# Dequantisation of three weight matrices ordered by matrix, on one core of a Trainium2

## What is computed

```python
BLOCKSIZE = 64
...
def nf4_quant_dequant(w):
    shape = w.shape
    flat = w.reshape(-1, BLOCKSIZE)
    absmax = jnp.max(jnp.abs(flat), axis=1, keepdims=True)
    normalized = flat / jnp.where(absmax == 0, 1.0, absmax)
    bounds = (NF4_CODE[:-1] + NF4_CODE[1:]) * 0.5
    idx = jnp.searchsorted(bounds, normalized)
    return (NF4_CODE[idx] * absmax).reshape(shape)
dq1 = nf4_quant_dequant(w1)
dq2 = nf4_quant_dequant(w2)
dq3 = nf4_quant_dequant(w3)
gate = jnp.einsum('bsd,hd->bsh', x, dq1)
up = jnp.einsum('bsd,hd->bsh', x, dq2)
h = jax.nn.silu(gate) * up
return jnp.einsum('bsh,dh->bsd', h, dq3)
```

## Time and profile before

| | |
|---|---|
| median of 3 runs (lowest to highest) | 1632.03 us (1629.77 to 1635.35) |
| the profiled execution: its own time | 1631.09 us |
| its span from first to last instruction | 1629.4 us |
| PE busy | 1390.0 us, 85% of the span |
| DVE busy | 1010.8 us, 62% |
| ACT, POOL busy | 461.3 us, 294.3 us |
| mean granted TensorE clock | 0.925 |

### The profile page before, as it was taken

The page is one execution under the profiler, slowest core; times in us unless marked ns, Lnnn a source line. Parts: engine busy times, 40 slices in busy tenths (PEclk is TensorE's granted clock), DMA queues, the critical chain, the costliest instruction groups (busy, mean ns, idle before and its releaser), DMA issues.

```text
span 1629.4 us, 18357 instructions
## 1 busy us (share of the span) xinstructions
PE 1390.0 (85%) x6285; PEld 1070.1 (66%) x6285; DVE 1010.8 (62%) x2281; ACT 461.3 (28%) x993; POOL 294.3 (18%) x170
## 2 busy tenths in 40 slices
PE   5559999999899988989967678589997777888998
PEld 5437776777677766867745467457886454677886
DVE  3657777767877765654596665854457399744141
ACT  3224334332333432313332103223212232321010
POOL 3101111111111111211112002115422311022110
PEclk9879999999999999999976789779998899899999
DMA  5521223313222321132101102100111100011001
GB/s 178 181 73 53 77 62 99 80 53 91 74 55 72 94 78 53 53 87 78 44 26 59 54 21 80 49 18 26 52 52 53 39 0 1 1 39 65 23 19 52
DMA packets 99405, 96.37 MB, mean 59 GB/s; under 512 B 13138, under 2 KB 72418, under 8 KB 99314
## 3 DMA queue, kind: packets, MB, share of 16 engines
q1 hardware_dynamic: 98802, 94.35, 19.8%
q0 software_dynamic: 512, 0.85, 0.2%
HBM read 84.34 MB, written 10.82 MB: 58 GB/s over the span
## 4 chain that ended last, share of the span: by engine, by line
PE 65%; DVE 23%; issue 5%; ACT 3%; DMA 2%; SPq 1%; POOL 1%; DVEq 0%; ACTq 0%; POOLq 0%
PE bank L1666 49%; PE bank L2033 6%; PE bank L1758 4%; DVE nf_y L1611 3%; DVE st L1174 2%; PE bank L1691 2%; DVE xn L1192 1%; PE bank L1748 1%; DVE mx L1528 1%; DMA nf_a<-in_L_w 1%; DVE xT L1151 1%; PE bank L1996 1%; DVE rt L1161 1%; SPq L771 1%; POOL slots L817 1%
## 5 line engine op out<-in xcount | busy, mean ns | idle before, releaser
L1666 PE MATMUL bank<-xT,slots 128*128 128x512 f32 (+1 forms) x1920 | 468.8, 402 | 12.3 <-DVE xT L1151 8.9
L1666 PEld LDWEIGHTS bank<-xT,slots 128*128 128x128 f32 (+1 forms) x1920 | 355.5, 186 | 111.6 <-issue 9.3
L817 POOL TENSOR_TENSOR slots<-staging,slots 128x1024 fp32r<-128x1024 f32 (+4 forms) x97 | 228.3, 2357 | 1063.9 <-ACT slots L910 1063.9
L1611 DVE TENSOR_SCALAR nf_y<-nf_w 128x512 fp32r<-128x512 f32 (+2 forms) x495 | 250.0, 532 | 38.4 <-PE bank L2033 37.2
L1666 PE MATMUL bank<-slots,h 128*128 128x512 f32 (+1 forms) x728 | 179.3, 406 | 15.9 <-DVE h L1284 9.7
L2033 PE MATMUL bank<-nf_y,nf_d 128*128 128x512 f32 (+2 forms) x495 | 165.3, 418 | 13.4 <-DVE nf_y L1611 11.3
L1666 PEld LDWEIGHTS bank<-slots,h 128*128 128x128 f32 (+1 forms) x728 | 141.1, 194 | 51.9 <-DVE h L1284 10.5
L910 ACT ACTIVATE slots<-staging 128x1024 fp32r<-128x1024 f32 (+4 forms) x97 | 98.2, 1018 | 188.6 <-PE bank L1666 175.6
L944 ACT ACTIVATE e<-bank,mx 128x320 f32<-128x320 f32 x128 | 66.4, 523 | 231.5 <-DVE mx L1229 217.9
L2033 PEld LDWEIGHTS bank<-nf_y,nf_d 128*128 128x128 f32 (+1 forms) x495 | 93.6, 194 | 50.4 <-issue 18.0
L1758 PE MATMUL bank<-eT,v 128*96 128x256 f32 (+1 forms) x384 | 108.6, 404 | 0.3
(11 more groups left out here) (246 smaller groups left out, 1716.1 us busy)
## 6 DMA issues: line engine op xcount, KB each, us to landing
staging<-in_L_wqkT SPq DMA_DIRECT2D x16, 480.0 KB, 3.9
nf_out<-nf_w SPq DMA_DIRECT2D x30, 256.0 KB, 2.1
staging<-nf_out SPq DMA_DIRECT2D x30, 256.0 KB, 2.9
staging<-in_L_woT SPq DMA_DIRECT2D x16, 384.0 KB, 3.7
staging<-in_L_w SPq DMA_DIRECT2D x12, 512.0 KB, 3.7
nf_a<-nf_max SPq DMA_DIRECT2D x40, 128.0 KB, 3.5
nf_r<-nf_rcp SPq DMA_DIRECT2D x40, 128.0 KB, 3.3
nf_w<-in_L_w SPq DMA_DIRECT2D x15, 256.0 KB, 4.2
```

The source lines that it names most:

```text
L817: g.tensor_tensor(lo, split_source(i), hi.bitcast(FP32), ALU.subtract).then_inc(*sig.mark("weight_low", i))
L1611: v.tensor_scalar(nf_y[0:rows, i % STAIR_RING, 0:size], w_, bound, first, compare, ALU.mult)\
L1666: ins = mm(dst, l_, r_, start=i == 0, stop=i == len(passes) - 1)
```

## The change

Only the 11 maxima of matrix 0 come first, then `nf_turn` 0 and item 0. The items run matrix by matrix (item n is matrix n // 11, block n % 11). From item 4 on, after its parts 4, 9 and 14, one entry of a second list is put in: the 11 maxima and the turn of matrix 1, then those of matrix 2. Their rows go through `xn[:, 0:3]` with waits three blocks back, their tables lie in `xn[:, 3]`. One copy per matrix is dropped (L1587), and the table is cleared per matrix. SP waits for the stored maxima of an item's own matrix. `stats` (1, 0) waits for the last tables to be stored.

```diff
--- before.py
+++ after.py
@@ -92,6 +92,7 @@
 STAIRS = staircase()
 NPART = len(STAIRS)
 STAIR_RING, STAIR_LAG = 6, 4
+REST_FROM = 4
 NF_BANK = 7
 
 
@@ -379,7 +380,7 @@
         nf_a = sb("nf_a", [P, 2, D], FP32, nfs)
         nf_r = sb("nf_r", [P, D], FP32, nfs)
         l = ExitStack()
-        nf_m = sb("nf_m", [P, 3, 88], FP32, l)
+        nf_m = sb("nf_m", [P, 2, 88], FP32, l)
         nf_t = sb("nf_t", [P, 2, P], FP32, l)
         l.close()
         nf_y = sb("nf_y", [P, STAIR_RING, D], F32R, nfs)
@@ -517,7 +518,7 @@
         def ffn_up(name, gate, up, lo, hi):
             for f in range(lo, hi):
                 w = fwidth(f)
-                chunk((name, f), P, (2, KT, w), [((0,), gate(f)), ((1,), up(f))], after=after_nf(name, 3 * f + 1))
+                chunk((name, f), P, (2, KT, w), [((0,), gate(f)), ((1,), up(f))], after=after_nf(name, FT + f))
 
         def ffn_down(name, down, lo, hi):
             for f in range(lo, hi, 2):
@@ -525,10 +526,10 @@
                 w = fwidth(f + n - 1)
                 if w == P or n == 1:
                     chunk((name, f), w, (n, D), [((i,), down(f + i, w)) for i in range(n)],
-                          after=after_nf(name, 3 * (f + n - 1) + 2))
+                          after=after_nf(name, 2 * FT + f + n - 1))
                 else:
-                    chunk((name, f), P, (1, D), [((0,), down(f, P))], after=after_nf(name, 3 * f + 2))
-                    chunk((name, f + 1), w, (1, D), [((0,), down(f + 1, w))], after=after_nf(name, 3 * f + 5))
+                    chunk((name, f), P, (1, D), [((0,), down(f, P))], after=after_nf(name, 2 * FT + f))
+                    chunk((name, f + 1), w, (1, D), [((0,), down(f + 1, w))], after=after_nf(name, 2 * FT + f + 1))
 
         def after_nf(name, item):
             return ("nf4_stored", item) if name in ("up3", "down3") else None
@@ -579,11 +580,13 @@
         base = schedule(only)
         if only is None or only == 7:
             jobs = []
-            for m in range(3):
+            jobs += [("nf_max", 0, f) for f in range(FT)] + [("nf_turn", 0)]
+            rest = []
+            for m in range(1, 3):
                 for f in range(FT):
-                    jobs += [("nf_max", m, f)] + [("nf_turn", m - 1)] * (m > 0 and f == 4)
-            jobs.append(("nf_turn", 2))
-            items = [(3 * f + m, m, f) for f in range(FT) for m in range(3)]
+                    rest.append(("nf_max", m, f))
+                rest.append(("nf_turn", m))
+            items = [(m * FT + f, m, f) for m in range(3) for f in range(FT)]
             jobs.append(("nf_load", *items[0]))
             sums = []
             for n, m, f in items:
@@ -600,8 +603,12 @@
                         jobs.append(("nf_store", *items[n - 1]))
                     if j == NPART // 2 + 1 and n + 1 < len(items):
                         jobs.append(("nf_load", *items[n + 1]))
+                    if n >= REST_FROM and j % 5 == 4 and rest:
+                        jobs.append(rest.pop(0))
             jobs += sums + [("nf_end", *items[-1]), ("nf_store", *items[-1])]
             base = with_background(base, "v0", BACKGROUND_END, jobs)
+            assert base.index(("turn", 0, 1)) < base.index(("nf_max", 1, 0))
+            assert base.index(("nf_turn", 2)) < base.index(("stats", 1, 0))
         steps = []
         if known:
             last = known.last_step
@@ -680,7 +687,21 @@
 
         def rows_buffer(i):
 
-            return (nf_w, nf_a)[i // 2 % 2][:, i % 2]
+
+
+            return (nf_w, nf_a)[i // 2 % 2][:, i % 2] if i < FT else xn[:, (i - FT) % 3]
+
+        def rows_loaded(i):
+
+            return f"nf4_rows{i % 4 if i < FT else 4 + (i - FT) % 3}"
+
+        def maxima(m):
+
+            return nf_m if m == 0 else xn[:, 3, 0:176].rearrange("p (a n) -> p a n", a=2)
+
+        def turned(m):
+
+            return nf_t if m == 0 else xn[:, 3, 176:432].rearrange("p (a n) -> p a n", a=2)
 
         def stair(n, j):
 
@@ -719,15 +740,17 @@
                 w = fwidth(f) if m < 2 else P
                 n = D if m < 2 or f < 10 else 6 * BLOCK
                 i = m * FT + f
-                if i >= 4:
-                    sp.wait_ge(*sig.when("nf4_max", divmod(i - 4, FT)))
+                if FT <= i < FT + 3:
+                    sp.wait_ge(*sig.when("turn_product", (0, 1, KT - 1)))
+                elif i >= 4:
+                    sp.wait_ge(*sig.when("nf4_max", divmod(i - (4 if i < FT else 3), FT)))
                 src = nf_src[m][f * P:f * P + w] if m < 2 else a["L3_w3"][:, f * D:f * D + n]
-                sp.dma_start(rows_buffer(i)[0:w, 0:n], src).then_inc(*sig.mark(f"nf4_rows{i % 4}", (m, f), 16))
+                sp.dma_start(rows_buffer(i)[0:w, 0:n], src).then_inc(*sig.mark(rows_loaded(i), (m, f), 16))
 
             def nf_turned(m):
                 for i, dst in enumerate((nf_max[m], nf_rcp[m])):
                     sp.wait_ge(*sig.when("nf4_turned", (m, i)))
-                    sp.dma_start(dst, nf_t[0:88, i]).then_inc(*sig.mark(f"nf4_maxima_stored{i}", m, 16))
+                    sp.dma_start(dst, turned(m)[0:88, i]).then_inc(*sig.mark(f"nf4_maxima_stored{i}", m, 16))
 
             def broadcast_rows(dst_tile, src, m, f):
 
@@ -755,10 +778,10 @@
             def nf_load(n, m, f):
                 w = fwidth(f)
                 rows, size = (P, KT * w) if m < 2 else (w, D)
-                if n == 0:
+                if f == 0:
                     for i in range(2):
-                        sp.wait_ge(*sig.when(f"nf4_maxima_stored{i}", 2))
-                else:
+                        sp.wait_ge(*sig.when(f"nf4_maxima_stored{i}", m))
+                if n:
                     sp.wait_ge(*sig.when("nf4_scaled", n - 1))
                 if n >= 2:
                     sp.wait_ge(*sig.when(f"nf4_stored{n % 2}", n - 2))
@@ -1117,11 +1140,11 @@
             def nf_turn(m):
                 for i in range(2):
                     act.wait_ge(*sig.when("nf4_turn_product", m))
-                    if m:
+                    if m > 1:
                         act.wait_ge(*sig.when(f"nf4_maxima_stored{i}", m - 1))
                     elif i == 0:
                         act.wait_ge(*sig.when("nf4_max", (0, 0)))
-                    sc.activation(nf_t[0:88, i], psum(("nf_turn", m))[0:88, i * P:(i + 1) * P], ACT.Copy)\
+                    sc.activation(turned(m)[0:88, i], psum(("nf_turn", m))[0:88, i * P:(i + 1) * P], ACT.Copy)\
                         .then_inc(*sig.mark("nf4_turned", (m, i)))
 
             handlers = {"split": split, "turn": turn, "v0": v0_, "k0": k0_, "kc0": kc0_, "q0": q0_, "scores0": scores0,
@@ -1188,6 +1211,9 @@
                 if layer or hf:
                     prev = (layer, 0, KT - 1) if hf else (layer - 1, 1, KT - 1)
                     dve.wait_ge(*sig.when("turn_product", prev))
+                if (layer, hf) == (1, 0):
+                    for i in range(2):
+                        dve.wait_ge(*sig.when(f"nf4_maxima_stored{i}", 2))
                 for t in ts:
                     v.tensor_scalar(xn[:, t % TPH], x[:, t], mv[:, t, 0:1], rs[:, t:t + 1], ALU.subtract, ALU.mult)\
                         .then_inc(*sig.mark("normalised", (layer, t)))
@@ -1574,19 +1600,17 @@
                 w = fwidth(f) if m < 2 else P
                 n = D if m < 2 or f < 10 else 6 * BLOCK
                 i = m * FT + f
-                dve.wait_ge(*sig.when(f"nf4_rows{i % 4}", (m, f)))
-                if (m, f) == (0, 0):
-                    link(v.memset(nf_m[:], 0.0))
-                v.tensor_reduce(nf_m[0:w, 0, f * 8:f * 8 + n // BLOCK], rows_buffer(i)[0:w, 0:n].rearrange("p (b k) -> p b k", k=BLOCK),
+                dve.wait_ge(*sig.when(rows_loaded(i), (m, f)))
+                if f == 0:
+                    if m > 1:
+                        dve.wait_ge(*sig.when("nf4_turn_product", m - 1))
+                    link(v.memset(maxima(m)[:, 0], 0.0))
+                v.tensor_reduce(maxima(m)[0:w, 0, f * 8:f * 8 + n // BLOCK], rows_buffer(i)[0:w, 0:n].rearrange("p (b k) -> p b k", k=BLOCK),
                                 AX.X, ALU.max, apply_absolute_value=True).then_inc(*sig.mark("nf4_max", (m, f)))
                 if f == FT - 1:
                     dve.wait_ge(*sig.when("nf4_max", (m, f)))
-                    c = 88 if m < 2 else 86
-                    if m:
-                        dve.wait_ge(*sig.when("nf4_turn_product", m - 1))
-                    link(v.tensor_copy(nf_m[:, 1, 0:88], nf_m[:, 0, 0:88]))
-                    link(v.tensor_scalar(nf_m[:, 2, 0:88], nf_m[:, 1, 0:88], TINY, None, ALU.max))
-                    v.reciprocal(nf_m[:, 2, 0:88], nf_m[:, 2, 0:88]).then_inc(*sig.mark("nf4_rcp", m))
+                    link(v.tensor_scalar(maxima(m)[:, 1], maxima(m)[:, 0], TINY, None, ALU.max))
+                    v.reciprocal(maxima(m)[:, 1], maxima(m)[:, 1]).then_inc(*sig.mark("nf4_rcp", m))
 
             def nf_stairs():
 
@@ -2019,7 +2043,7 @@
```

(2 more changed lines are left out.)

## The result

The changed kernel takes 1649.19 us (median of 4 runs, 1646.25 to 1650.66); the kernel before took 1630.9 beside it. The ratio is 1.0107, with a 95% interval of 1.0083 to 1.0132: slower by 17 to 18 us; the profiled spans differ by 17.0, 1629.4 to 1646.4.

What follows compares the result with a forecast made beforehand. PE bounds the attention stage; from 40 to 120 us it idles 34.5 us, waiting for DVE. The terms, -14.5 + 8 - 1 + 14 = 6.5, taken as 6, give 1637.1 us profiled, 1638.0 median; range 1622 to 1650.

Steps and rivals of the forecast that it cites:

- the forecast case: Whole kernel: the predicted outcome, slower at 1638.0 us; case 1634 to 1645 with chance 0.43, own range 1632 to 1645.
- term 2: Units 12 to 36: DVE waits for late row loads, mostly borne; 8 us more, bounds 0 to 25.
- Term 1: The start, before unit 12: early idle time of PE, then fewer waits and sums done ahead; 14.5 us less, bounds 8 to 20.
- the faster case: Rival: start gives 19 as PE keeps its clock, term 2 is 2, Term 3 is 10; -7, 1625 us, chance 0.23.
- The wait behind `stats` (0, 1): At the start: PE's idle time of 8.6 us there falls to 3 to 4, since PE has other work.
- The eight waits behind `nf_store`: Items 4 to 11, maximum after part 4: its load follows the store; DVE idles 2 to 4 us each, 16 to 25 in sum.
- An item's two other row loads go out early and are hidden.: Units 12 to 36: row loads other than that of the maximum after part 4 cause no waits.
- a third of the waits as the cost: Units 12 to 36: most DVE waits for rows are borne, as seven `nf_r` waits were; 8 us of at most 25.
- "1 us less" for the long loads that leave: Attention stage: long loads of matrix 2 leave it with their waits; 1 us less.
- My own mark: Sign, units 12 to 36: PE busy less than 185 of 200 us would mean term 2 was too small.
- Term 3: First `down0` pass: items 24 to 26 all need long loads of matrix 2; 14 us more, bounds 10 to 17.
- the third rival: Units 12 to 36: DVE becomes the bound as waits of maxima meet splits; +18 us in all, 1650 us, chance 0.12.

## Why the prediction came out as it did

Slower was forecast, and slower it is, by 17 us where the forecast had 6. The measured time lies at the upper end of the range and above the forecast case's own, 1632 to 1645. Nearly all of the difference is term 2's; the other differences, -1.0 us at the start, -1.0 between unit 63 and item 23, -1.3 in the pass and +3.8 behind it, happen to cancel. By the steps:

**Term 1, the start: right in its sum, not in its parts.** Forecast -14.5, measured -15.5 at unit 11; kernels alike up to there lie between -12.7 and -17.5. PE idles 11.54 us at the turn (forecast 10.6), the first item starts at 56.9 (58.2 to 58.8), PE is busy 60.0 of 80 us (55), at a clock of 0.82. That was more than I had taken, and nearly the mark at which I had put the faster case; it was worth 1 us more, not 4.5. But the scores of unit 6 end at 109.2, where the forecast had 113 (before: 115.0), and from there to unit 11 the gain is 9.7 us, not 12.5. The wait behind `stats` (0, 1) is 6.28 us and not 3 to 4, and the one of 11.08 us before, which the prediction does not name, fell by 7.5. That the sum fits within 1 us is in part luck.

**Term 2, units 12 to 36: its mechanism was half seen, and its size was wrong.** Forecast +8 with bounds 0 to 25, less 1; measured +19.7 at unit 38, +17.0 at unit 63. The eight waits behind `nf_store` were forecast as 16 to 25 us in sum and came to 23.0. The step that failed is the sentence "An item's two other row loads go out early and are hidden." They go out when SP comes to them, and SP stands behind chunk loads that wait for splits; six waits with 27.4 us are theirs, and three of the eight are longer by the same cause. The second error was to take a third of the waits as the cost, going by seven borne waits for `nf_r`. Those were borne indeed, by the run with fewer DMAs in the kernel before, but the waits for rows are not of their kind: by the runs with all, some and no such waits they cost a half, part of it as lower clock. The third has the other sign: "1 us less" for the long loads that leave was 4.3 from unit 11 on by the run with the order alone, though by that same run not for the issue of these loads. With the rows ahead, units 11 to 63 change by -10.9 (those 4.3, and 6.6 that were not parted from the compare steps that moved to the start); the waits add 27.9 and so make the measured +17.0. My own mark was PE busy less than 185 of 200 us; it is 184.1.

**Term 3, the first pass: right.** Forecast +14, measured +12.7, and 14.8 and 12.5 in the runs of the order alone and of the rows ahead. Waits of DVE of 6.74, 8.19 and 9.19 us (forecast 8 to 12), of PE of 3.33, 4.69 and 1.69 (two of about 5). That the issue of the DMAs is the cause was argued then; two runs that shorten it in different ways, by 13.3 us each beyond unit 63, show it. Behind item 27 another 3.8 us are lost, and between 0.9 and 5.2 in the other kernels with this order, 3.6 even with few DMAs. "Longer loads elsewhere are hidden" may have failed there; what these us are was not tried.

**The rivals.** The time is that of the third rival, 1650 us, but not by its mechanism. DVE does not become the bound: its work in 183 to 383 us, 126.5 us, and 42 us of waits for rows stay 15 us below PE's 184. That count came out as forecast, but it is not what decides: single waits of 4 to 7 us were longer than the work PE had at hand. That the maxima meet splits is excluded as the cause by the run with the same maxima and no waits.

## What to carry to other kernels

When a load lands is set by its place in its queue as much as by its own length: before calling one hidden, write down what stands ahead of it on the issuing engine, and what that waits for. Give loads their own places in the order, ahead of their readers; here that alone turned 1.1% slower into 0.4% faster. Where an item needs twenty small DMAs, count their issue as work of an engine (0.6 us each here), and share it with another engine or make the transfers fewer before changing the order of the items.

## What the runs showed that was not expected

POOL issues a broadcast of 16 or 32 KB in 0.54 to 0.58 us, no slower than SP. A us of DVE's waits for rows cost the program half a us, in three amounts (0, 28.7 and 50.4 us), and nearly half of that cost was the clock: 0.94 instead of 0.99 over 270 us, though PE was idle only 20.5 of them. The waits for `nf_r` in attention, 18 us of them less, brought nothing behind unit 11, so the price of a wait is not one number. And of three long loads moved into units 38 to 57, one cost 9.1 us, one 4.3 and one nothing, which no average of PE's load would tell.
